# One core: attention sums kept by feature and divided per batch, with the first 20 tiles' output products moved into the attention's last stage

## What is computed

```python
x = x + 0.5 * ffn(layernorm(x), ...)
# attention
score = jnp.einsum('bqd,bkd->bqk', rope(q), rope(k))      # causal
attn  = softmax(score / sqrt(8))
out   = jnp.einsum('bqk,bkd->bqd', attn, v)               # 64 (batch, head) pairs
x = x + heads_joined(out) @ Wo.T
x = x + 0.5 * ffn(layernorm(x), ...)
```

## Time and profile before

| | |
|---|---|
| median of 3 runs | 800.54 us (800.43 to 805.24) |
| profiled execution | 801.62 us, of which the profile's span is 799.6 us |
| TensorE busy | 751.4 us, 94% of the span |
| VectorE busy | 609.3 us, 76% |
| ScalarE busy | 506.8 us, 63% |
| GpSimd busy | 313.9 us, 39% |

### The profile page before, as it was taken

The page is one execution under the profiler, slowest core; times in us unless marked ns, Lnnn a source line. Parts: engine busy times, 40 slices in busy tenths (PEclk is TensorE's granted clock), DMA queues, the critical chain, the costliest instruction groups (busy, mean ns, idle before and its releaser), DMA issues. The chain is left out here.

```text
span 799.6 us, 17942 instructions
## 1 busy us (share of the span) xinstructions
PE 751.4 (94%) x5618; PEld 438.9 (55%) x5618; DVE 609.3 (76%) x1919; ACT 506.8 (63%) x1229; POOL 313.9 (39%) x603
## 2 busy tenths in 40 slices
PE   9899999888999999999999999999999978699994
PEld 8888997455434344434433443334344337688994
DVE  5757774499999898889889888988898508746663
ACT  2156662486267787778777877787787762156662
POOL 6077744176423223322422342233223310175753
PEclk8599999999999999999999999999999999689998
DMA  8822212127642133123303321332130000321110
GB/s 261 312 54 52 57 36 93 45 80 184 159 75 37 27 60 62 28 35 61 58 16 51 62 44 20 62 60 37 27 61 4 2 6 31 119 56 40 52 39 27
DMA packets 27989, 51.84 MB, mean 65 GB/s; under 512 B 7552, under 2 KB 19200, under 8 KB 26496
## 3 DMA queue, kind: packets, MB, share of 16 engines
q1 hardware_dynamic: 21296, 41.04, 22.1%
q0 software_dynamic: 4096, 8.69, 4.2%
q10 hardware_dynamic: 2512, 1.06, 0.5%
HBM read 35.40 MB, written 14.97 MB: 63 GB/s over the span
## 5 line engine op out<-in xcount | busy, mean ns | idle before, releaser
L1411 DVE CUSTOM_DVE_ANT_0 cst<-psS,mask_row 128x768 bf16<-128x768 f32 (+7 forms) x512 | 362.1, 756 | 41.5 <-PE psS L1284 37.4
L1374 ACT ACTIVATE prob<-psST 128x512 f32<-128x512 f32 (+3 forms) x750 | 320.2, 498 | 107.9 <-PE psST L1316 86.9
L1331 PE MATMUL a_psO<-prob,vs 128*32 128x512 f32 (+3 forms) x1536 | 157.5, 496 | 0.4 <-ACT p_anT L1380 0.2
L1482 POOL TENSOR_TENSOR a_gate<-a_zeros 1x1 f32<-1x1 f32 x128 | 23.4, 183 | 290.7 <-ACT prob L1374 290.5
L1316 PE MATMUL psST<-a_qs,ks 75*128 75x512 bf16 (+1 forms) x480 | 125.8, 328 | 0.0
L1284 PE MATMUL psS<-ks,a_qs 72*128 72x512 bf16 (+2 forms) x480 | 112.4, 326 | 0.1
L777 POOL DMA_INDIRECT tok<-rows,f_there_number x64 | 61.7, 964 | 86.4 <-DVE f_number L489 42.6
L1316 PEld LDWEIGHTS psST<-a_qs,ks 75*128 75x128 bf16 x480 | 42.7, 97 | 80.5 <-ACT prob L1374 50.4
L1483 POOL TENSOR_SCALAR_AFFINE_SELECT prob<-prob 128x512 f32<-128x512 f32 x128 | 79.9, 624 | 0.0
L1316 PE MATMUL psST<-qs,ks 75*128 75x512 bf16 (+3 forms) x270 | 71.8, 328 | 0.1
L1284 PE MATMUL psS<-ks,qs 72*128 72x512 bf16 (+3 forms) x288 | 67.8, 327 | 0.6 <-DVE a_rowmax L1411 0.3
(11 more groups left out here) (185 smaller groups left out, 1080.4 us busy)
## 6 DMA issues: line engine op xcount, KB each, us to landing
a_qs<-q_split SPq DMA_DIRECT2D x60, 96.0 KB
rows<-tok SPq DMA_DIRECT2D x8, 536.0 KB, 5.1
ks<-k_split SPq DMA_DIRECT2D x32, 128.0 KB
qs<-q_split SPq DMA_DIRECT2D x36, 96.0 KB
q_split<-p_part SPq DMA_DIRECT2D x24, 128.0 KB, 2.4
k_split<-p_part SPq DMA_DIRECT2D x24, 128.0 KB, 2.4
ks<-k_split SPq DMA_DIRECT2D x16, 192.0 KB
tok<-x_after_first SPq DMA_DIRECT2D x4, 536.0 KB, 5.2
```

The costliest lines, as they stand in the source:

```text
L1331: last = nc.tensor.matmul(psO[32 * h:32 * h + 32, c0:c0 + w], vs[r][:, j, h, :], prob[:, u % RING, h, 0:w], start=(j == 0), stop=(u + 1 in ...
L1374: nc.scalar.activation(prob[:, u % RING, h, 0:w], score_buffer(s, u * QH + h)[:, 0:w], ACT.Exp, scale=SCALE).then_inc(exp_done, 1)
L1411: last = nc.vector.tensor_tensor_reduce(out=out[:, a * CH:a * CH + width], in0=ps[:, a * CH:a * CH + width], in1=mask_row[:, S - width:], ...
```

## The change

The sums stay in rows of features, and the division is made once per batch and half.

- The value tensor `vs` carries eight columns of ones per head instead of one, so `psO` holds each head's sum of exponentials in eight rows, one for each feature.
- ScalarE copies `psO` to `outT`, now with two buffers, one per half. SyncE then moves it in eight DMAs per half, each of 8 rows of 512 numbers (16 KB): for each head the sums of exponentials to `weight_sums` (the tensors `p_an0` and `p_an1`) and the outputs to `shared`, which now has features in its rows. These DMAs count on the semaphores `kept0` and `kept1`, one for each half.
- When the four stages of a batch are done, VectorE takes the reciprocal of `weight_sums`, 128x512 per half (`invert`), and GpSimd multiplies it into `shared` (`divide`). In stages 4, 8 and 12 this stands behind tile 4 (half 0) and tile 5 (half 1) in VectorE's program. For the last batch half 0 stands at the end of the attention, half 1 at the start of the second block.
- The transposes `A` and `B` with VectorE's two instructions are gone, and so are the transposes and copies at the start of the second block: `shared` is already turned.
- `LAST` has ten letters `p`. Each makes the output products of two tiles (20 tiles in all), VectorE's additions and their statistics. The second block does the other 12 tiles, three groups.
- The strings of letters were written anew; a middle stage has 86 letters instead of 88.

```diff
-        link(nc.gpsimd.memset(n.vs[r][:, :, :, DK + 1:], 0.0))
-        link(nc.gpsimd.memset(n.vs[r][:, :, :, DK:DK + 1], 1.0))
+        link(nc.gpsimd.memset(n.vs[r][:, :, :, 2 * DK:], 0.0))
+        link(nc.gpsimd.memset(n.vs[r][:, :, :, DK:2 * DK], 1.0))
...
-                for t in range(NT):
+                for t in range(LATE_TILES if r == 1 else 0, NT):
...
+            if r == 1:
+                invert(dve, n, B - 1, 1)
             statistics()
...
+def invert(dve, n, b, ch):
+
+    dve.wait_ge(n.kept[ch], 2 * QH * 16 * (b + 1) * (H // QH))
+    dve.reciprocal(n.weight_sums[ch], n.weight_sums[ch]).then_inc(n.inverted, 1)
+
+
+def divide(pool, n, b, ch):
+
+    pool.wait_ge(n.inverted, b * NCH + ch + 1)
+    rows = n.shared[:, b * TB + ch * CB:b * TB + (ch + 1) * CB, :].rearrange("p n d -> p (n d)")
+    pool.tensor_tensor(rows, rows, n.weight_sums[ch], ALU.mult).then_inc(n.divided, 1)
...
-    LAST = ("ssswswssssNsswssssswssssswwssssssBssswssswsssswsssswsssswssssAwww")
+    LAST = ("spsswwsssssNpspsspsswwssssspssswwsspsssspsswwsssssswwssssspsspsswsssspwww")
...
+    INVERT_AFTER = (4, 5)
+    OWN_MASKS = 1
...
+        def keep(s, ch):
+
+            sp.wait_ge(out_copied, 2 * s + ch + 1)
+            if s % QB == 0:
+                wait(sp, n.divided, (s // QB - 1) * NCH + ch + 1)
+            for h in range(QH):
+                rows = slice(s % QB * RW + h * DK, s % QB * RW + (h + 1) * DK)
+                sp.dma_start(weight_sums[ch][rows, :],
+                             outT[ch][32 * h + DK:32 * h + 2 * DK, :]).then_inc(n.kept[ch], 16)
+                sp.dma_start(attended[rows, ds(s // QB * S + ch * CH, CH)],
+                             outT[ch][32 * h:32 * h + DK, :]).then_inc(n.kept[ch], 16)
 
         def stage(s):
             if s > 0:
                 load_max(s, s % RING, 1)
             if s > 0 and s + 2 < NST:
                 load(s + 2, (s + 2) % RING)
+            if s > 0:
+                keep(s - 1, 1)
+            keep(s, 0)
...
-        def turn_out(s, ch, index, ps):
+        def project(p, index, ps):
 
             use(index)
-            pe.wait_ge(out_copied, 2 * s + ch + 1)
-            for b in range(CB):
-                last = nc.tensor.transpose(ps[:, b * P:(b + 1) * P], outT[:, b * P:(b + 1) * P], n.c("ident"))
+            wait(pe, n.divided, 2 * p // CB + 1)
+            for j in range(2):
+                last = nc.tensor.matmul(ps[:, j * WIDE:(j + 1) * WIDE], n.shared[:, 2 * p + j, :], n.out_and_router,
+                                        start=True, stop=True)
             last.then_inc(use_done, 1)
...
+        def add_project(p, index, ps):
...
+            nc.vector.tensor_tensor(n.early[:, tiles_, :], n.early[:, tiles_, :], both[:, :, D:], ALU.add)
+            nc.vector.tensor_tensor(n.tok[:, tiles_, 0:D], n.tok[:, tiles_, 0:D], both[:, :, 0:D],
+                                    ALU.add).then_inc(use_read, 1)
+            dve.wait_ge(use_read, index + 1)
+            for t in range(2 * p, 2 * p + 2):
+                nc.vector.bn_stats(n.tok[:, t, D:], n.tok[:, t, 0:D]).then_inc(added, 1)
...
+                if s % QB == 0 and s > 0 and what == "tile" and arg in INVERT_AFTER:
+                    invert(dve, n, s // QB - 1, INVERT_AFTER.index(arg))
 
         run(stage)
+        invert(dve, n, B - 1, 0)
+        dve.wait_ge(added, 1 + LATE_TILES)
...
                     values(s + 1, (s + 1) % RING)
+                    if s % QB == 0 and s > 0:
+                        for ch in range(NCH):
+                            divide(pool, n, s // QB - 1, ch)
```

More of the change, by code:

```diff
@@ L212, in build @@
         with nc.Block() as block:
+            n.kept, n.inverted, n.divided = [sem(f"kept{i}") for i in range(NCH)], sem("inverted"), sem("divided")
             n.scattered = ffn(nc, n, block, 0, n.x_dram)
@@ L609, in _ @@
             else:
-                turn(True, 0)
-                turn(True, 1)
-                for g in range(G):
+                for g in range(LATE_TILES // CB, G):
                     project(g)
-                    if g + 2 < G:
-                        turn(True, g + 2)
             warm_up(nc, pe, n, psW, FILL[0][r])
@@ L702, in _ @@
                 if u >= XT:
-                    _, _, read, count = turns[u - XT]
+                    _, read, count = turns[u - XT]
                     act.wait_ge(read, count)
@@ L1210, in attention @@
     outT = n.outT
-    recip = [n.mean[:, i * CB * QH:(i + 1) * CB * QH].rearrange("p (b h) -> p b h", b=CB) for i in range(NCH)]
     psO = psum("psO", CH)
@@ L1502, in _ @@
         run(stage)
+        divide(pool, n, B - 1, 0)
 _OUT = (B, S, D)
```

92 lines of the change are left out of this document (43 added, 49 removed).

## The result

The changed kernel takes 859.8 us (median of four, 857.73 to 862.33), the kernel before 801.8 (median of four). The ratio is 1.071, with an interval of 1.068 to 1.075. The forecast was 830 us, with a range up to 850: the direction and the place were right, the size was half of what came. The profiled execution took 858.99 us, of which 857.2 are the span, 57.6 more than before.

The account below looks back on a forecast made before the run. TensorE was taken as the bound in the attention's middle stages, ScalarE in the last, VectorE after it. 801.6 + 49.8 - 12.8 - 7.3 = 831.3, given as 830 us because the median run is 1.1 below the profiled one; range 804 to 850.

Parts of the forecast that it names:

- first stop, tile 6: Stages 4, 8, 12: half 0's reciprocal delays the copy of turn N, so tile 6 starts 2.4 us late on TensorE.
- landing of `kept1`, stage 4: Stage 4: SyncE's eight transfers, issued behind ten loads, land at 350.3 us; VectorE waits for them before the second reciprocal.
- second stop, tile 8, stage 4: TensorE stands ahead of tile 8 from 342.1 to 354.8 us, until VectorE has reduced tile 6: 12.7 us.
- clock, per slow stage: Stages 4, 8, 12: five microseconds near half speed after a stall cost 2.5 us, bounds 0 and 5.
- a slow stage in all, mean of three: Stages 4, 8 and 12 each lose 2.4 + 12.7 + 2.5 - 1.0 = 16.6 us, the three 49.8.
- gain per ordinary stage: First and middle stages: four transposes removed per half-stage free 0.44 us of TensorE each, 29 x 0.44 = 12.8 us in all.
- end of the attention to the end of the statistics: Last stage and second block: 20 tiles' additions and statistics move into the attention, three groups remain; gain 7.3 us.
- two corrections: Stages 4, 8, 12, beyond the stalls: lower clock costs 2.5 us, emptied ScalarE gives 1.0 us back.
- rival 3: Removed transposes were not on TensorE's path, so 12.8 us are not gained: 843 us, chance 0.15.
- rival 1: Middle stages' new order takes away half of TensorE's 6.9 us of waits: 782 us, chance 0.08, plus 0.05 for only offsetting stalls.
- rival 4: Stages 4, 8, 12: queue slower than priced, high ends of landing and clock, 22.5 us per stage: 848 us, chance 0.10.
- block's change of 3.0 us: End of attention: the next block starts 3.0 us after GpSimd's product, 657.6 to 660.6 us.

Follow-up runs that it names:

- e3_first_only: Changed kernel with only the second reciprocal of stages 4, 8 and 12 moved, to behind tile 16; the first stays behind tile 4: 837.2 us (one run).
- e7_spread: Changed kernel with each reciprocal in four 128-column pieces, half 0's in stages 4, 8, 12, half 1's in the next stages, GpSimd's products at their ends: 935.8 us, 1.163.
- e1_late: Changed kernel with the two reciprocals of stages 4, 8 and 12 behind tiles 10 and 16 instead of 4 and 5: 822.9 us, ratio 1.025.
- e5_busy_long: Changed kernel with throw-away matmuls on TensorE ahead of tiles 6 and 8 of stages 4, 8 and 12, 17 rounds of four before tile 8: 840.1 us (one run).

## Why the prediction failed in size

| term | forecast | measured |
|---|---|---|
| reciprocal of 128x512 | 3.2 us | 3.35 |
| first stop, tile 6 | 2.4 | 2.20 |
| landing of `kept1`, stage 4 | 350.3 | 352.94 |
| second stop, tile 8, stage 4 | 12.7 | 14.75 |
| beyond the stops, with the clock at 1.00 | -1.0 | +1.5 |
| clock, per slow stage | 2.5 | 5.8 |
| a slow stage in all, mean of three | 16.6 | 24.1 |
| gain per ordinary stage | 0.88 | 0.63 |
| end of the attention to the end of the statistics | -7.3 | -3.7 |
| behind the statistics | 0 | -3.5 |

**Right**: the mechanism, its places and its order. The reciprocal's price from two short rows was good to 5% (353 + 480 x 6.1 ns is 3.28 us, not the 3.2 written). (The estimate from the Trainium skill, VectorE: DVE Perf Modes, section "First, the fixed hardware budget", was 4.3 us; the 3.35 measured decide.) Both stops are there, released by what was named. TensorE's waits for VectorE show them in all three stages, where the kernel before has none (us in total, times, longest):

```profile
PE psS L1312 <- DVE a_rowmax L1440: 44.0, 3, 15.0
PE psS L1312 <- DVE a_maxT L1448: 6.5, 3, 2.2
```

That is 16.8 us per stage against the forecast 15.1.

**The step that failed** is the "two corrections". Of the 22.5 us missing in the three stages, the clock is 3 x 3.3. I took 5 us near half speed from the one pause in the trace, with an upper bound of 5 us lost; behind the long wait the clock stayed low for 17, 11 and 11 us of work in the three stages, and the 5.8 us are above even that bound. The correction next to it had the wrong sign: ScalarE, empty after the stop, was expected to give back 1.0 us, but with the clock held at 1.00 a stage still lost 1.5 us more than the stops of the changed kernel (18.3 against 16.8). Of that 0.7 is that the stops themselves are longer there (17.5), and the other 0.8 stays unexplained; a part may be the throw-away products. Nothing came back. That is 3 x 2.5. The stops are the last 3 x 1.7: eight issues were priced at 0.31 us, the smallest loads', but a transfer from SBUF takes 0.62 to 0.70 on this queue, 2.9 us more for the eight; and the landing took 2.9 us instead of 2.4. (Stage 4 starts 0.5 us earlier in this trace, so `kept1` landed 3.1 us late, not 2.6; TensorE stopped 1.2 us later than forecast, which leaves the 2 us of the table.) The row to take stood in the same group: the maxima, also a transfer from SBUF, at 0.70. (That the source makes the price is a guess; no run varies it alone.)

**Near number, wrong reason**: the ordinary stages. TensorE without a gap was taken as the sign that its transposes were on the path, and rival 3 got 0.15. It was true: in the old order removing them gave 0.08 us, and the loads waited for ScalarE instead, as the earlier trace rows had said. The new order gave 0.55, in time a small piece of rival 1, but not by its mechanism: the loads' waits are 8.8 us in the new order (6.4 and 2.4) against 6.9 before. The two together gave 9.2 us in 14 stages and stage 0, against 12.8.

**Luck**: rivals 3 and 4 together, the pair that the range left out, say 861 us, next to the 859.8. Rival 3 was right on the transposes and rival 4 on the queue and the clock, but the slow stages cost 24.1 us each, more than rival 4's 22.5, and the ordinary stages gained 9.2 us where rival 3 had them gain nothing.

**The end.** The working up to GpSimd's product was good (53.0 us behind stage 14's start, forecast 52.7), and so were the three groups of 1.72 us behind the second reciprocal. The block's change of 3.0 us was not transferable: it came behind a VectorE instruction, and here behind a GpSimd product, which took 5.57. The 3.5 us gained behind the statistics nobody had forecast; they go with the clock. The same ten microseconds behind the end of the statistics, in the kernel before, in the changed one and in e3_first_only:

```profile
700.00:710.00 10.00, 8.71 (x45) 8.08 (x46) 2.94 (x12) 4.98 (x14) 7.56 (x9) 0.62 0.25 56
```

```profile
761.10:771.10 10.00, 8.76 (x69) 8.04 (x70) 5.25 (x22) 6.63 (x18) 7.56 (x9) 1.00 0.24 55
```

```profile
736.30:746.30 10.00, 8.83 (x49) 8.40 (x50) 3.31 (x14) 5.27 (x14) 7.56 (x9) 0.62 0.23 55
```

From the end of the statistics to the end of the span the first takes 123.3 us, the second 119.7 and the third 122.8, though its second block is that of the second. In the 13 other traces, all at 0.98 or more in this stretch, it is 119.6 to 120.7. So this gain is not a sure one of the change, and why the clock comes back later in some executions is open.

Together: 22.5 (slow stages) + 3.6 (ordinary ones) + 0.1 (3.6 less at the end, 3.5 more behind it) + 1.7 (scatter of the first part) + 1.9 (the medians against the profiled executions, 0.8 and 1.1) = 29.8, the distance from 830 to 859.8.

## What to carry over

When an engine that feeds TensorE gets a long instruction, ask how long TensorE stands behind it, and price the work after the stop at the lower clock as well as the stop; the same work in pieces that fit into the engine's waits cost next to nothing here. For every transfer that is added to a queue, take the issue time of a row with the same kind of source, and for every semaphore that a queue waits on, look at what stands behind it: one such wait made e7_spread 132 us slower. And an engine without a gap does not prove that each of its instructions is on the path, if its loads wait for another engine all the time.

## What the runs showed of the hardware

- A stop of TensorE of 2.2 us was followed by 26 us of work at a granted clock of 0.50 (e3_first_only, stage 4), one of 2.9 us by 10 us at 0.52 (e1_late, stage 4), and one of 2.1 us by none (the changed kernel, stage 12). With throw-away products in the stops it stayed at 1.00 (e5_busy_long). What decides whether it falls and how long it stays low was not settled.
- SyncE's issue of an 8x512 transfer from SBUF takes 0.62 us (median of 128 each of two kinds), twice the 0.31 of the smallest load.
- With a product of GpSimd near the end of a block, the next block began 5.56 to 5.57 us behind that product in three traces. The mechanism behind this number was not looked into.
